# Attention stage of an AdaLN, attention, GRU and FFN kernel: scores ahead of y's transposes, block selection on ScalarE, x loaded per tile, steps of the projection and the statistics moved

## What is computed

```python
x = x + attn(cond(x, ...), W_attn, b_attn, W_proj, b_proj)
x = x + ffn(gru(cond_2048, x, W_ih, W_hh, b_ih, b_hh), weight, scale_weight, bias)

# cond: per batch row, sums over 8 blocks of 4 steps; keys = sums @ Wk.T, RMS-normalised;
#   softmax over the 8 blocks of keys . q; attended = weighted sum of the block sums;
#   y = layernorm(x + attended @ Wo.T) * gamma + beta      (the same row for all 32 steps)
# attn: 32 heads of 8 features, causal with ALiBi; out = softmax(q k / sqrt(8)) v @ W_proj + b_proj
# gru: 32 steps in sequence over the batch; ffn: x @ (weight * scale).T + bias
```

## Time and profile before

| what | us |
|---|---|
| median of three runs | 441.64 (440.5 to 442.12) |
| the profiled execution | 443.33 |
| its span, first to last instruction | 441.5 |
| attention stage, first `probs_v` to the end of the last | 50.7 to 254.8 |
| granted clock of TensorE, mean of the span | 0.987 |

### The profile page before, as it was taken

The page is one execution under the profiler, slowest core; times in us unless marked ns, Lnnn a source line. Parts: engine busy times, 40 slices in busy tenths (PEclk is TensorE's granted clock), DMA queues, the critical chain, the costliest instruction groups (busy, mean ns, idle before and its releaser), DMA issues.

```text
span 441.5 us, 14915 instructions
## 1 busy us (share of the span) xinstructions
PE 404.9 (92%) x6216; PEld 339.8 (77%) x6216; DVE 330.7 (75%) x971; ACT 221.1 (50%) x545; POOL 141.4 (32%) x202
## 2 busy tenths in 40 slices
PE   8799799997999899888888699999999999999994
PEld 6557586775877778567676598899999999999984
DVE  3587789899898998949669844677667777777665
ACT  6254457565575665636565453444444444444341
POOL 7673256564365546435468500000000000000000
PEclk9999899999999999989999999999999999999999
DMA  7952313222123322412113000000000000000001
GB/s 287 394 189 83 110 51 88 85 91 82 51 86 93 91 76 75 122 38 64 49 51 100 3 1 0 1 21 29 26 24 25 25 24 26 26 24 26 24 26 71
DMA packets 33251, 30.46 MB, mean 69 GB/s; under 512 B 3104, under 2 KB 28320, under 8 KB 33184
## 3 DMA queue, kind: packets, MB, share of 16 engines
q1 hardware_dynamic: 33184, 29.51, 20.0%
HBM read 16.92 MB, written 8.39 MB: 57 GB/s over the span
## 4 chain that ended last, share of the span: by engine, by line
PE 66%; DVE 19%; issue 8%; ACT 5%; POOL 1%; DVEq 0%; POOLq 0%
PE ps_s L1452 7%; PE ps_t L1452 6%; PE ps_o L1452 6%; PE ps_s L1521 5%; PE ps_s L1351 5%; PE ps_t L1521 5%; DVE pT L976 5%; PE ps_a L1521 4%; PE ps_m L1389 4%; PE ps_m L1521 4%; PE ps_t L1279 4%; PE ps_o L1369 3%; DVE mx L968 3%; PE ps_a L1279 3%; PE ps_t L1288 2%
## 5 line engine op out<-in xcount | busy, mean ns | idle before, releaser
L534 POOL TENSOR_TENSOR sc<-masked,mx 128x512 f32<-128x512 f32 x64 | 66.2, 1056 | 93.3 <-DVE mx L968 93.3
L640 ACT ACTIVATE sc<-sc 128x512 f32<-128x512 f32 x64 | 40.1, 626 | 17.0 <-POOL sc L534 17.0
L960 DVE COPY_PREDICATED masked<-kst,ps_s 128x512 f32<-128x512 int32 x64 | 44.2, 740 | 3.1 <-PE ps_s L1351 3.1
L1351 PE MATMUL ps_s<-kbd,qn 32*32 32x128 f32 x2048 | 39.1, 277 | 5.9 <-issue 5.8
L976 DVE STREAM_TRANSPOSE pT<-sc 128x512 f32<-128x512 f32 x64 | 41.5, 684 | 1.0 <-ACT sc L640 0.8
L754 ACT ACTIVATE zg<-ps_t,brz 128x128 f32<-128x128 f32 x64 | 20.1, 365 | 39.6 <-PE ps_t L1452 37.3
L968 DVE TENSOR_REDUCE mx<-masked 128x16 f32<-128x512 f32 x64 | 39.9, 664 | 0.0
L1389 PEld LDWEIGHTS ps_m<-oT,w_p 128*128 128x128 f32 x256 | 33.5, 198 | 7.6 <-ACT oT L573 6.3
L1389 PE MATMUL ps_m<-oT,w_p 128*128 128x128 f32 x256 | 36.2, 286 | 2.8 <-ACT oT L573 2.8
L1113 DVE SCALAR_TENSOR_TENSOR rg<-ps_o,vec,rg 128x128 f32<-128x128 f32 x64 | 19.5, 346 | 24.8 <-PE ps_o L1452 23.8
L1452 PEld LDWEIGHTS ps_s<-hT,w_hh 128*128 128x128 f32 x256 | 33.4, 193 | 5.0 <-DVE hT L1131 2.8
(11 more groups left out here) (165 smaller groups left out, 825.6 us busy)
## 6 DMA issues: line engine op xcount, KB each, us to landing
xf<-in_x_feat SPq DMA_DIRECT2D x8, 512.0 KB, 9.5
xg<-in_x_tok SPq DMA_DIRECT2D x8, 512.0 KB, 4.0
kbd<-kn SPq DMA_DIRECT2D x64, 64.0 KB, 2.1
v_dram<-vn SPq DMA_DIRECT2D x16, 256.0 KB, 3.1
vbd<-v_dram SPq DMA_DIRECT2D x64, 64.0 KB, 2.1
out_feat<-ost SPq DMA_DIRECT2D x16, 256.0 KB, 2.0
w_qkv<-in_wqkv SPq DMA_DIRECT2D x1, 768.0 KB, 9.7
w_ih<-in_wih SPq DMA_DIRECT2D x1, 768.0 KB, 13.3
```

Source lines behind the costliest of these rows:

```text
L534: nc.gpsimd.tensor_tensor(shifted, kept, m.unsqueeze(2).to_broadcast([P, NH // 2, S]), ALU.subtract).then_inc(sc_sub, 1)
L640: nc.scalar.activation(part, part, ACT.Exp).then_inc(sc_exp, 1)
L960: nc.vector.copy_predicated(kept, keep.unsqueeze(1).to_broadcast([P, NH // 2, S]), ps_s[:, h * 512:(h + 1) * 512].rearrange("p (h k) -> p ...
L1351: last = nc.tensor.matmul(ps_s[head * S:(head + 1) * S, out_col:out_col + KH * S], qn[rows, g % 2, c, cols], kbd[rows, g % 2, c, :, cols], ...
```

## The change

Six edits to the order, on every engine. PE makes the scores of tile n + 1 ahead of `transpose_y`. `select_blocks` for groups 2 to 7 moves from DVE to ACT, behind the first exponential of step one, and ACT copies the attention output between the two halves of `round_y`. SP loads x for group g + 2 in four DMAs of 128 KB, three of them in step one and the last one once the scores of the next step are done. `spread_proj` and `add_proj` move from step three to step two (for g > 0), the statistics all to the end of step three, so that `transpose_probs` of step four now stands behind the mask. The chain of groups 5 to 7 moves from steps one and two of the third group to its steps three and four, with `cond_sums` and `cond_mean` from step one to the end of step two. In the first group the second half of the keys moves from step two to step one. POOL's `rest_of_gru_weights` in the seventh group moves from the end of a step to its start.

```diff
+CHAIN_AT = ((0, 0), (2, 2))
+CHAIN_END = ((0, 1), (2, 3))
...
                     sp.wait_ge(z_done, 2 * g + 4)
-                    sp.dma_start(xg[:, :, :], x_group(g + 2)).then_inc(l_xg, DMA)
+                    for tile in range(GT):
+                        if tile > 0:
+                            sp.wait_ge(sc_mm, GT * g + 2 + tile // 3)
+                        sp.dma_start(xg[:, tile, :], x_tok[GT * (g + 2) + tile]).then_inc(l_xg, DMA)
...
-                    if i == 0 and g == 2:
+                    if i == 2 and g == 2:
                         inverse_rms(3)
+                    if g == NG - 2 and i > 0:
+                        rest_of_gru_weights(i - 1)
...
-                    if g == NG - 2 and i > 0:
-                        rest_of_gru_weights(i - 1)
...
+            def select_blocks(k):
+
+                act.wait_ge(weights_kept, 1 if k < 5 else 2)
+                act.wait_ge(proj_mm, k)
+                nc.scalar.activation(ra[:, :], member, ACT.Identity, scale=wcol[:, k:k + 1]).then_inc(ra_ready, 1)
...
                 softmax_exp(n, n % 2, 0)
+                if i == 0 and 0 < g < NG - 2:
+                    select_blocks(g + 2)
                 if i == 0 and not last_group:
                     round_y(g + 1, 0)
-                    round_y(g + 1, 1)
-                    softmax_exp(n, n % 2, 1)
                 if n > 0:
                     attn_out(n - 1)
-                if i > 0 or last_group:
-                    softmax_exp(n, n % 2, 1)
+                if i == 0 and not last_group:
+                    round_y(g + 1, 1)
+                softmax_exp(n, n % 2, 1)
...
-                if i == 0 and g in (0, 2):
+                if (g, i) in CHAIN_AT:
                     cond_exp(2 + g // 2)
...
                 if i == 1 and g == 0:
-                    round_proj(g + 2, proj_ps)
+                    select_blocks(2)
+                    round_proj(2, proj_ps)
...
                 if h == 0:
-                    dve.wait_ge(l_xg, DMA * (k + 1))
+                    dve.wait_ge(l_xg, DMA * (k + 1 if k < 2 else 2 + GT * (k - 1)))
...
-                if i == 0 and 0 < g < NG - 2:
-                    select_blocks(g + 2)
-                if i == 0 and g + 5 < NG:
-                    cond_sums(g + 5)
-                if i == 0 and g == 2:
-                    cond_mean(3)
-                if i == 1 and g in (0, 2):
+                if (g, i) in CHAIN_END:
                     cond_normalise(2 + g // 2)
-                if i == 0 and g + 1 < NG:
-                    rest_of_y(g + 1)
-                if norm_ahead and i == 3:
-                    some_token_stats(g + 2, 1).then_inc(bn_done, 1)
-                    mean_and_variance(g + 2)
+                if g == 0 and i == 3:
+                    some_token_stats(2, 1).then_inc(bn_done, 1)
+                    mean_and_variance(2)
                     transpose_probs(n, n % 2)
                 if n + 1 < NT:
                     softmax_mask(n + 1, (n + 1) % 2)
-                if i == 0 and g == 2:
+                if i == 0 and g + 1 < NG:
+                    rest_of_y(g + 1)
+                if (g, i) == (2, 2):
                     cond_scores(3)
-                if i == 0 and g in (0, 2):
+                if (g, i) in CHAIN_AT:
                     cond_shift(2 + g // 2)
+                if (g, i) in CHAIN_END:
+                    keep_weights(2 + g // 2)
+                if g > 0 or i < 3:
+                    transpose_probs(n, n % 2)
                 if i == 0 and 0 < g < NG - 2:
                     rest_of_proj(g + 2, proj_ps_ahead)
-                if i == 1 and g in (0, 2):
-                    keep_weights(2 + g // 2)
-                if not norm_ahead or i < 3:
-                    transpose_probs(n, n % 2)
-                if i == 1 and g == 0:
-                    select_blocks(2)
-                if norm_ahead and i == 2:
+                if norm_ahead and i == (1 if g > 0 else 2):
                     add_proj(g + 2, ps_a)
                 if n + 1 < NT:
                     softmax_max(n + 1, (n + 1) % 2)
-                if norm_ahead and i == 2:
-                    some_token_stats(g + 2, 0)
+                if g == 0 and i == 2:
+                    some_token_stats(2, 0)
+                if 0 < g < NG - 2 and i == 2:
+                    token_stats(g + 2)
+                    mean_and_variance(g + 2)
+                if i == 1 and g + 5 < NG:
+                    cond_sums(g + 5)
+                if i == 1 and g == 2:
+                    cond_mean(3)
...
+                if n + 1 < NT:
+                    scores(n + 1, (n + 1) // GT, (n + 1) % GT)
                 if i == 0 and not last_group:
                     transpose_y(g + 1)
-                if n + 1 < NT:
-                    scores(n + 1, (n + 1) // GT, (n + 1) % GT)
...
-                if norm_ahead and i == 2:
+                if g == 0 and i == 2:
                     pe.wait_ge(k_out, 2 * g + 4)
-                    spread_proj(g + 2, ps_a)
-                if i == 1 and g in (0, 2):
+                    spread_proj(2, ps_a)
+                if (g, i) in CHAIN_END:
                     cond_col(2 + g // 2)
-                if i == 1 and not last_group:
+                if i == 1 and 0 < g < NG - 1:
                     keys(g + 1, 1)
...
-                if i == 0 and g in (0, 2):
+                if (g, i) in CHAIN_AT:
                     cond_row(2 + g // 2)
                 if i == 0 and not last_group:
                     keys(g + 1, 0)
+                if n == 0:
+                    keys(1, 1)
+                if i == 1 and 0 < g < NG - 2:
+                    pe.wait_ge(k_out, 2 * g + 4)
+                    spread_proj(g + 2, ps_a)
                 if i == 1 and not last_group:
                     queries(g + 1, 0)
...
-                if i == 0 and g in (0, 2):
+                if (g, i) in CHAIN_AT:
                     pe.wait_ge(c_sub, 3 + g // 2)
-                if i == 1 and g in (0, 2):
+                if (g, i) in CHAIN_END:
                     pe.wait_ge(weights_kept, 1 + g // 2)
```

More of the change, by code:

```diff
@@ L855, in select_blocks @@
             def select_blocks(k):
[L857 to L863 removed]
+                dve.wait_ge(c_col, k + 1)
+                nc.vector.tensor_scalar(ra[:, :], member, ps_o[:, 320 + P:321 + P], None, ALU.mult).then_inc(ra_ready, 1)
             def rest_of_proj(k, bank):
```

7 lines of the change are left out of this document (removed).

## The result

The changed kernel takes 446.92 us (median of 4 runs, 444.2 to 448.95); the kernel before took 441.88 beside it (4 runs, 440.5 to 443.52). The ratio is 1.0126 (95% interval 1.0073 to 1.018): **1.3% slower**, where 435.3 and "faster" had been forecast. Ratios leave disturbed executions out, so one need not be the exact quotient of two medians.

What follows compares the result with a forecast made beforehand. TensorE and VectorE were taken as both nearly full in the attention stage. Order -3.3 (groups -2.2 + 0.2 + 1.0 - 1.0 - 1.3) and x per tile -3.0 made -6.3, so 441.6 to 435.3 us; range 430.5 to 441.0.

Steps and rivals of the forecast that it cites:

- The order of a quiet group: Steps one to four of a quiet group: -1.3 + 1.2 - 0.5 + 0.25 = -0.35 us.
- The chain in step three: Third group: VectorE waits with cond_shift about 1.7 us for a row product behind the output projection; group +1.0.
- The x pieces: x loads of 128 KB: each taken to land in 2.6 us, with no wait of the addition.
- -3.0: Sixth group, step two: splitting the x load removes most of a 4.7 us excess from a held-up instruction page.
- Rival B: Fetch stall isn't the x load's or comes back elsewhere: 438.3 us; chance 0.22.
- scores first: Step one: next tile's scores ahead of y's transposes run inside the wait for y; -1.3 us a quiet group.
- `cond_sums` at the end of step two, partly exposed: Second group: this, plus block products without slack in step four, turns -0.35 into +0.2 us.
- -2.2: First group: second half of the keys fills a wait of probs_v; net -2.2 us, between -0.5 and -3.
- The 0.95 taken off VectorE is worth nothing by itself: Step one: moving the selection off VectorE gains nothing alone, as VectorE then waits for ACT's second rounding.
- no more than about 1.4 us a group can be won by better order alone: Quiet group of 25.3 us: TensorE busy 23.9 limits what reordering can win to about 1.4 us.
- +1.2 ... -0.5 ... +0.25: Moving spread, addition and statistics: step two +1.2, step three -0.5, step four +0.25 us a quiet group.
- Rival D: Page fetch moves behind fourth x piece and kbd loads; slower, two more stalls give 447.7 us; chance 0.11.

Runs made afterwards that it cites:

- the best order, pages back: The best order with TensorE's 16 warm-up products made into 8 twice as wide, 32 instructions fewer, so pages end 16 products later; 437.23 us, ratio 0.9948.
- the best order: Changed kernel with cond_sums before step two's addition, spread, addition and statistics back in steps three and four, chain's row product before output projection; 438.52 us, ratio 0.9966.

## Why the prediction was wrong

**Right.** *The order of a quiet group*: -0.39 measured, -0.35 predicted, and each step within 0.25. `probs_v` of tile 1 at 57.52 (near 57). *The chain in step three*: 1.79 of wait for the row product (1.7). *The x pieces*: 2.4 to land (2.6 taken), and no wait of the addition on a DMA.

**The step that failed first: "-3.0" as a reading of the earlier trace rows, "TensorE's next page of instructions held up behind the x load".** A lone packet of the instruction queue behind a load was taken for cause and effect. It was a page, and TensorE waited for it, but the stop is tied to product 39 of tile 22, and both the stop and the late packet stay with no x load at all (2.12, the packet 4.8 after the end of the page before). For the term of 3.0 the runs show nothing that can be told from zero: the sixth group won 1.4 in all, and one load in place of four pieces was 0.4% slower, with overlapping intervals. Rival B said just that ("isn't the x load's or comes back elsewhere"), and had 0.22. What neither it nor the forecast saw is that *scores first* itself makes pages' ends tell: `probs_v` and the scores, 256 instructions with their weight loads, now follow each other in step one as they do elsewhere, so that TensorE is through a page sooner: it took 3.4 for the one that ends in tile 17, and the packet of the next had ended only 3.7 after that page began. The fifth group, counted at -0.35, got two standstills (1.87 and 1.25) and lost 2.1. The sixth got one in y's transposes, behind the scores of tile 21 (1.86), kept its low clock (0.94) and won 1.4, not 3.35; the seventh lost its full clock.

**The second: "`cond_sums` at the end of step two, partly exposed", inside "+0.2" for the second group.** Together with the block products of step four it had been given 0.55 (from -0.35 to +0.2). Put directly behind the maximum, they run beside the subtraction that the maximum starts, at 0.90 and 1.25 in place of 0.39 and 0.43, and with `normalise` queued behind them TensorE waited up to 2.3. Moving them a few positions gave 5.2 us back in the median, 2.3 in the profile. The same coincidence was in the earlier trace rows, which the prediction used: the selection took 0.95 on VectorE, for 48 columns, and ended as POOL's subtraction did.

**The third: "-2.2" for the first group.** Step two lost 1.43, about as priced, and then step three went from 6.42 to 7.77: 0.63 of wait for `normalise` and 0.52 at a page's end. With neither it takes 6.39 (the best order, pages back). The earlier start of the first `probs_v` was 0.17, not 0.5.

**Also wrong, at no cost to the sum: "The 0.95 taken off VectorE is worth nothing by itself"**. The earlier trace rows had VectorE busy for 8.00 of the 8.24, and with the selection left on it step one stays at 8.53 with scores first (VectorE busy for 8.06). And "no more than about 1.4 us a group can be won by better order alone" took TensorE's busy time for a floor; the best order won 1.5 in the quiet group.

**Sized right, judged wrong: "+1.2 ... -0.5 ... +0.25" for the move of the spread.** Steps two to four came out at +1.19, -0.43 and +0.31 against the kernel before, and step one at -1.48 ("-1.3"). But the order without the move shows that the two parts share these sums otherwise than the prediction had it: scores first and the selection bring 2.1 in step one and cost 0.6 in step two, and the move takes 0.65 of step one back as well. It cost 1.1 of 1.5 in every quiet group, and undoing it gave 5.6 us. The prediction had put it at +0.95 and summed on. Since the forecast counted it, it is not part of the distance between forecast and result; it is most of what made the change a loss.

The forecast was -6.35 by groups; the profile had +1.66 up to the last `probs_v`. The 8.0 between them: first group 1.8, second and third 1.8, fifth 2.5, sixth 1.9, seventh 0.4, eighth -0.4. That places the distance in the profiled execution; it does not price each cause, since a stop and another wait can stand in for one another. The median is 2.7 above it, at lower clocks, and that this comes of falls of the clock behind more standstills is argued from the runs' clocks, not shown. Rival D had the number (447.7) by luck: it put a page's fetch behind the x pieces and `kbd`; the x pieces were excluded, `kbd` loads were not tried, and the sums and the spread, which give back 5.2 and 5.6, were not in it.

Open also: what makes a page's packet come late, about 1 after the page before has ended in most cases and up to 6.0 in others, and what the stops cost the kernel as a whole.

## What to carry to other kernels

Before a VectorE instruction is moved, look at what GpSimd does in its new place: the same instruction can take two to three times as long beside it, and whatever stands behind it on the queue pays. A stop put down to issue should be counted in instructions before it is explained by a transfer that happens to run: if it keeps its place in the list while times shift, it is the list's. Then set it beside the packets of the instruction queue, and take the suspected load away. An engine that is full in a step (VectorE, 8.00 of 8.24) keeps the step long whatever is won on another one. And when a change is a bundle, price each part for being left out; here one part took back three quarters of what another had won.

## What the runs showed of the hardware

VectorE beside GpSimd (POOL in the rows): the products with accumulation (128x256) took 0.37 to 0.43 alone, and beside GpSimd's subtraction 0.88 to 0.91 (L819) and 1.25 or 1.26 (L821) in every trace of that order. The selection (128x48) took 0.94 or 0.95 beside it and 0.19 at the least. To overlap is not enough, though. With the sums back in step one, the first product began just ahead of GpSimd's two additions. It took 0.41, and the additions 1.41, where a pair takes 1.0 elsewhere. The profile of that kernel:

```profile
75.20 0.41 DVE L819 CUSTOM_DVE_ANT_0 junk<-kw_ahead 128x256 f32<-128x256 f32 x1
...
75.29 1.41 POOL L547 TENSOR_TENSOR xf<-xo,xf 128x128 f32<-128x128 f32 x2
```

So either engine can be the one that waits. The Trainium skill (Advanced Engine Details and Errata, VectorE Performance Modes) says that VectorE's second SBUF port is shared with GpSimd, and that GpSimd's instructions and VectorE's two-port ones block each other. These durations agree; whether the products here count as two-port instructions no run shows.

TensorE's instructions come in packets of 16 KB, one for each 256. Where it stopped at a page's end (for 0.3 to 3.2 us, mostly inside or right behind runs of small products, 128 instructions in 0.8 to 1.15 us), it went on 1.15 to 1.59 after the end of a packet; at most other pages' ends nothing was seen. The Trainium skill (Runtime: NRT & Kernel Launch, Instruction fetch mechanics) calls the crossing "mostly hidden". By count the traces agree, with three to ten visible stops for 49 or 50 packets; by time they don't, with 5 to 14 us of TensorE waiting at pages' ends (waits of 0.3 and more) in the attention stage of each profile.

Tiny products are not cheap everywhere: 64 of them took 8.48 us in the load phase and 32 took 3.68 ahead of the first group, where the 64 of a scores run take 1.15. Why is not shown.
